# Turning the token rows on VectorE, in blocks of quarter rows, in a gated attention and mixture-of-experts layer on one core

## What is computed

```python
router_logits = flat @ router_w.T
probs = jax.nn.softmax(router_logits, axis=-1)
topk_w, topk_idx = jax.lax.top_k(probs, TOP_K)          # TOP_K = 2 of E = 16 experts
topk_w = topk_w / jnp.sum(topk_w, axis=-1, keepdims=True)
shared = silu(flat @ shared_gate_w) * (flat @ shared_up_w) @ shared_down_w      # F_SH = 1024
...
g = jax.lax.ragged_dot(xs, gate_w, group_sizes)         # D = 1024 -> F_EXP = 512
u = jax.lax.ragged_dot(xs, up_w, group_sizes)
h = silu(g) * u
dn = jax.lax.ragged_dot(h, down_w, group_sizes)         # 512 -> 1024
routed = zeros_like(flat).at[sorted_tok].add(sorted_w[:, None] * dn)
output = shared + routed
```

## Time and profile before

| | |
|---|---|
| median of 3 executions | 3086.06 us |
| the profiled execution, on the device | 3110.33 us |
| its span, from the first to the last instruction | 3108.8 us |
| PE busy | 2960.7 us (95%) |
| DVE busy | 1638.6 us (53%) |
| ACT busy | 1013.8 us (33%) |
| POOL busy | 595.8 us (19%) |
| mean granted TensorE clock | 0.979 of full speed |

### The profile page before, as it was taken

How to read it: one execution, slowest core, us unless ns; L and a number is a source line. 1 busy time by engine, 2 the same in 40 slices (tenths; PEclk the granted TensorE clock), 3 DMA queues, 4 the chain that set the end, 5 groups by cost and what they waited for, 6 DMA issues and landing times.

```text
span 3108.8 us, 48018 instructions
## 1 busy us (share of the span) xinstructions
PE 2960.7 (95%) x17262; PEld 2443.7 (79%) x17263; DVE 1638.6 (53%) x3104; ACT 1013.8 (33%) x1916; POOL 595.8 (19%) x572
## 2 busy tenths in 40 slices
PE   4799999999999988999999999999999999999999
PEld 3687777777878766888888888888888888888887
DVE  3778788887888764333243333332333344444444
ACT  4444444444444412332233333332333331111111
POOL 1333333333343331000000000000000001111111
PEclk6799999999999998999999999999999999999999
DMA  6454445445444534143433333433333324444444
GB/s 192 137 170 137 150 137 176 151 140 158 152 150 142 153 128 152 59 149 128 142 141 136 142 135 142 142 135 142 140 143 135 135 81 158 145 138 159 142 145 145
DMA packets 205721, 441.74 MB, mean 142 GB/s; under 512 B 86784, under 2 KB 87680, under 8 KB 205056
## 3 DMA queue, kind: packets, MB, share of 16 engines
q1 hardware_dynamic: 110544, 333.62, 31.7%
q0 software_dynamic: 24400, 72.96, 7.2%
q10 hardware_dynamic: 70656, 33.56, 4.2%
HBM read 350.72 MB, written 107.18 MB: 147 GB/s over the span
## 4 chain that ended last, share of the span: by engine, by line
PE 59%; DVE 1%; ACT 1%; ACTq 0%; issue 0%; DVEq 0%
PE p_g_b L1532 19%; PE p_up_b L1532 19%; PE p_y_b L1520 17%; PE p_x_b L1500 3%; PE p_h_b L1507 1%; DVE w_lo L1384 1%; ACT w_hi L1327 1%; ACTq L1181 0%; ACTq L1166 0%; DVE x L1440 0%; DVE sg_b L1412 0%; DVE x L1431 0%; ACT th_b L1369 0%; DVE y_b L1442 0%; ACTq L1323 0%
## 5 line engine op out<-in xcount | busy, mean ns | idle before, releaser
L1400 DVE TENSOR_TENSOR ht_lo_b<-p_h_b,ht_hi_b 128x512 fp32r<-128x512 f32 x105 | 72.4, 689 | 544.5 <-ACT ht_hi_b L1339 544.5
L1532 PE MATMUL p_g_b<-w_hi,xt_hi_b 128*128 128x512 f32 x840 | 342.0, 407 | 16.2 <-DVE w_lo L1384 12.9
L1520 PE MATMUL p_y_b<-w_hi,ht_hi_b 128*128 128x512 f32 x840 | 340.1, 405 | 1.9 <-DVE ht_lo_b L1400 1.9
L1412 DVE SCALAR_TENSOR_TENSOR sg_b<-th_b,p_g_b 128x512 f32<-128x512 f32 x105 | 72.1, 687 | 493.5 <-ACT th_b L1369 493.5
L1532 PE MATMUL p_up_b<-w_hi,xt_lo_b 128*128 128x512 f32 x840 | 331.0, 394 | 0.0
L1532 PE MATMUL p_up_b<-w_lo,xt_hi_b 128*128 128x512 f32 x840 | 330.1, 393 | 0.0
L1520 PE MATMUL p_y_b<-w_lo,ht_hi_b 128*128 128x512 f32 x840 | 330.0, 393 | 0.0
L1532 PE MATMUL p_g_b<-w_hi,xt_lo_b 128*128 128x512 f32 x840 | 329.8, 393 | 0.0
L1532 PE MATMUL p_up_b<-w_hi,xt_hi_b 128*128 128x512 f32 x840 | 327.4, 390 | 0.0
L1532 PE MATMUL p_g_b<-w_lo,xt_hi_b 128*128 128x512 f32 x840 | 327.0, 389 | 0.0
L1520 PE MATMUL p_y_b<-w_hi,ht_lo_b 128*128 128x512 f32 x840 | 326.8, 389 | 0.0
(11 more groups left out here) (221 smaller groups left out, 5694.1 us busy)
## 6 DMA issues: line engine op xcount, KB each, us to landing
mid_y<-y_b SPq DMA_DIRECT2D x73, 512.0 KB, 3.2
stage<-mid_g_row SPq DMA_DIRECT2D x64, 512.0 KB, 5.4
stage<-in_eg SPq DMA_DIRECT2D x16, 2048.0 KB
stage<-in_eu SPq DMA_DIRECT2D x16, 2048.0 KB, 15.2
stage<-in_ed SPq DMA_DIRECT2D x16, 2048.0 KB, 19.4
mid_y<-in_x SPq DMA_DIRECT2D x34, 512.0 KB
stage<-in_x SPq DMA_DIRECT2D x32, 512.0 KB
stage<-in_ctx_t ACTq DMA_DIRECT2D x32, 512.0 KB, 8.3
```

Of the source, the lines that this page charges most:

```text
L1400: nc.vector.tensor_tensor(ht_lo[:, :, :], p_h[:, :, :], ht_hi[:, :, :].bitcast(f32), ALU.subtract).then_inc(ht_rdy, 1)
L1412: nc.vector.scalar_tensor_tensor(out=sg[:, :], in0=th[:, :], scalar=1.0, in1=p_g[:, :], op0=ALU.add, op1=ALU.mult).then_inc(silu_step, 1)
L1520: last = nc.tensor.matmul(p_y[n][:, :], a[:, k, :], b[:, GUP + k, w], start=(k == 0 and m == 0), stop=(k == FE // P - 1 and m == 2))
L1532: mm = nc.tensor.matmul(out[:, :], a[:, k, :], w[:, k, o:o + FE], start=(k == 0 and m == 0), stop=(k == KD - 1 and m == 2))
```

## The change

**x.** The eight transposes of PE per tile are gone. A tile's rows are laid in `xg` as quarter rows: the 32 partitions of group a hold quarter a (256 floats) of all 128 tokens, four tokens to a partition. One instruction of DVE (`turn_x`) then turns 32 x 32 blocks inside each group of partitions into a new SBUF tile `x_t`, which is whole. Its row p of block k is column 8p + k of x, so the weights are loaded in the same order ("(p k)" in place of "(k p)"). `x_high` and `x_low` read `x_t` in place of PSUM.

**Gathering x.** POOL loads the numbers of the tokens four times (once for each group of partitions, 32 x 4 numbers), adds 0 to 3 to four times the token's number (`idx_q`; the lists now hold four times the number), and issues four indirect DMAs of 128 quarter rows of 1 KB. The plain loads of x are four DMAs of 32 partitions each (`quarters_in`).

**h.** The gated rows go to memory and back: ACT stores `h` to a DRAM buffer `mid_h` (`h_store`), waits for the store, loads it in the layout of quarters (`h_quarters`), DVE turns it (`turn_h`, in place of PE's), and ACT and DVE split it. Only the very last tile's h is still turned by PE.

**y.** Both halves of y are copied at the start of the next `body` (`y_of`), behind `split_gu` where a tile is an expert's first.

```diff
-        eng.dma_start(place, matrix.rearrange("(k p) f -> p k f", p=P)).then_inc(sem, 16)
+        eng.dma_start(place, matrix.rearrange("(p k) f -> p k f", p=P)).then_inc(sem, 16)
...
+        xn_quarters = t["xn"].rearrange("(c j t) (a d) -> c a j t d", t=4, j=32, a=4)
+        xn_flat = t["xn"].rearrange("c (a d) -> (c a) d", a=4)
+        xg_parts = xg[:, :].rearrange("p (t d) -> p t d", t=4)
+
+        def quarters_in(eng, c, done):
+
+            for a in range(4):
+                eng.dma_start(xg_parts[32 * a:32 * a + 32, :, :], xn_quarters[c, a]).then_inc(done, 16)
...
             def load_x(c):
-                sp.wait_ge(xt_ps, before + c)
-                sp.dma_start(xg[:, :], xn_rows[c]).then_inc(xs_in, 16)
+                sp.wait_ge(x_turned, before + c)
+                quarters_in(sp, c, xs_in)
...
-                    ge_apart(pool, past, (x_in, 16 * i))
-                    pool.dma_start(idx[:, :], list_parts[bass.ds(part, 1)].rearrange("o p w -> (o p) w")
-                                   ).then_inc(idx_in, 16)
-
-                ge_apart(pool, past, (idx_in, 16 * i + 16 if c is None else 0), (xt_ps, i))
+                    for a in range(4):
+                        pool.dma_start(idx[32 * a:32 * a + 32, :],
+                                       list_parts[bass.ds(part, 1)].rearrange("o (j t) w -> (o j) (t w)", t=4)
+                                       ).then_inc(idx_in, 16)
+                    ge_apart(pool, past, (idx_in, 64 * i + 64))
+                    ge_apart(pool, past, (x_in, 64 * i))
+                    nc.gpsimd.tensor_tensor(idx_q[:, :], idx[:, :], quarter[:, :], ALU.add).then_inc(idx_rdy, 1)
+                    ge_apart(pool, past, (idx_rdy, i + 1))
+                ge_apart(pool, past, (x_turned, i))
...
+                    for n in range(4):
+                        nc.gpsimd.indirect_dma_start(
+                            out=xg_parts[:, n, :], out_offset=None, in_=xn_flat,
+                            in_offset=bass.IndirectOffsetOnAxis(ap=idx_q[:, n:n + 1], axis=0)).then_inc(x_in, 16)
...
                 for p in range(GUP):
+                    if p == 3:
+                        h_quarters(i)
                     nc.scalar.activation(w_hi[:, p, :], stage[:, p, :], ACT.Copy).then_inc(gu_hi, 1)
...
+            def h_store(i):
+
+                act.wait_ge(h_rdy, i)
+                act.dma_start(t["h"].rearrange("a s f -> s a f"), h[:, :].rearrange("p (a f) -> p a f", a=4)
+                              ).then_inc(hs_out, 16)
+
+            def h_quarters(i):
+
+                act.wait_ge(hs_out, 16 * i)
+                act.dma_start(h[:, :], t["h"].rearrange("a (j t) f -> (a j) (t f)", t=4)).then_inc(hq_in, 16)
...
+            def y_of(q):
+
+                act.wait_ge(y_out, 16 * q)
                 act.wait_ge(y_ps, 2 * q)
-                nc.scalar.activation(y[:, 512:D], p_y[1][:, :], ACT.Copy).then_inc(y_rdy, 1)
+                for n in range(2):
+                    nc.scalar.activation(y[:, 512 * n:512 * n + 512], p_y[n][:, :], ACT.Copy).then_inc(y_rdy, 1)
...
                 if not (isinstance(i, int) and i < 2) and (c is None or isinstance(c, int) and c < 2):
-                    y_right(q)
+                    y_of(q)
                 if prev:
-                    h_high(i)
+                    if not first:
+                        h_quarters(i)
+                    h_high(i, q)
                 act.wait_ge(gu_ps, i + 1)
                 nc.scalar.activation(th[:, :], p_g[:, :], ACT.Tanh, scale=0.5).then_inc(tanh_rdy, 1)
                 if not last:
                     x_high(i + 1)
-                if prev == "routed":
-                    y_left(q)
+                    h_store(i + 1)
                 if first:
                     split_d(i, e, prev)
...
+            def turn_h(i):
+
+                dve.wait_ge(xt_rdy, 2 * i)
+                dve.wait_ge(hq_in, 16 * i)
+                nc.vector.transpose(h_t[:, :, :].rearrange("p k (j t) -> p t k j", t=4),
+                                    h[:, :].rearrange("p (t i k) -> p t k i", t=4, k=FE // P)).then_inc(h_turned, 1)
...
+            def turn_x(i, c):
+
+                ge(dve, xt_rdy, 2 * i)
+                if c is None or isinstance(c, int) and c == 0:
+                    dve.wait_ge(x_in, 64 * i + 64)
+                else:
+                    dve.wait_ge(xs_in, 64 * c)
+                nc.vector.transpose(x_t[:, :, :].rearrange("p k (j t) -> p t k j", t=4),
+                                    xg_parts[:, :, :].rearrange("p t (i k) -> p t k i", k=KD)).then_inc(x_turned, 1)
...
                 if prev:
-                    h_low(i)
+                    turn_h(i)
+                    h_low(i, h_t)
+                if not last:
+                    turn_x(i + 1, c)
                 silu_up(i)
...
-                    if k == 3 and prev:
-                        turn_h(i)
                 mm.then_inc(gu_ps, 1)
-                if not last:
-                    turn_x(i + 1, c)
                 if prev:
                     down(i, e - 1 if first else e)
```

More of the change, by code:

```diff
@@ L166, in mix_block @@
         cnt_ps, cnt_step = sem("cnt_ps"), sem("cnt_step")
-        idx, idx_in, row0_in = keep["idx"], keep["idx0_in"], keep["row0_in"]
+        idx, idx_q, quarter = keep["idx"], keep["idx_q"], keep["quarter"]
+        idx_in, idx_rdy, row0_in = keep["idx0_in"], keep["idx0_rdy"], keep["row0_in"]
         gu0_hi, gu0_split = keep["gu0_hi"], keep["gu0_split"]
         xn_out = sem("xn_out")
-        fill_in = sem("fill_in")
+        fill_in, quarter_set = sem("fill_in"), sem("quarter_set")
         wp_in = [sem(f"wp_in{n}") for n in range(SLOTS)]
@@ L1131, in ffn_block @@
         base_row = sb("base_row", [P, D])
-        p_x = [ctx.enter_context(nc.psum_tensor(f"p_x{n}_{tag}", [P, 4, P], f32)) for n in range(2)]
         p_g = ctx.enter_context(nc.psum_tensor(f"p_g_{tag}", [P, FE], f32))
@@ L1137, in ffn_block @@
         r0, r1 = keep["x1"][:, 0, :], keep["x1"][:, 1, :]
-        idx, starts_i = keep["idx"], keep["starts_i"]
+        idx, idx_q, quarter, starts_i = keep["idx"], keep["idx_q"], keep["quarter"], keep["starts_i"]
         first_row = sb("first_row", [P, NE])
@@ L1295, in gather @@
                     own = start(pool, NE)
-                    pool.wait_ge(y_out, 16 * own)
+                    pool.wait_ge(y_out, 16 * own + 16)
                     for n in range(2):
@@ L1377, in _ @@
             x_high(0)
-            tiles(act, body, lambda i, q, e, c: h_high(i))
+            tiles(act, body, lambda i, q, e, c: last_high(i))
         @block.vector
@@ L1490, in _ @@
             trio = ((xt_hi, w_hi), (xt_lo, w_hi), (xt_hi, w_lo))
-            def turn_x(i, c):
-                if c is None or isinstance(c, int) and c == 0:
-                    pe.wait_ge(x_in, 16 * i + 16)
-                else:
-                    pe.wait_ge(xs_in, 16 * c)
-                for k in range(KD):
-                    last = nc.tensor.transpose(p_x[k // 4][:, k % 4, :], xg[:, k * P:(k + 1) * P], ident[:, :])
-                last.then_inc(xt_ps, 1)
             def turn_h(i):
@@ L1506, in turn_h @@
                 for k in range(FE // P):
-                    last = nc.tensor.transpose(p_h[:, k, :], h[:, k * P:(k + 1) * P], ident[:, :])
+                    last = nc.tensor.transpose(p_h[:, k, :], h[:, k:FE:FE // P], ident[:, :])
                 last.then_inc(ht_ps, 1)
```

78 lines of the change are left out of this document (45 added, 33 removed).

## The result

The changed kernel takes **3050.6 us** (median of 4 runs, 3043.6 to 3054.7) against 3085.0 us for the kernel before beside it (3082.6 to 3086.2): ratio 0.989, 95% interval 0.9878 to 0.9902. It is faster by 34 us (30 to 38), where 146 were forecast and 2940 us, and the range (2930 to 2990) does not hold it.

A forecast was written before the change was run, and what follows sets the result against it. PE, busy 95% of the span, was taken as the bound. Savings of 89.6 us (x), 45.8 (h) and 12.9 (changes of expert), less 2 (start), made 146 us off the 3086.1 median: 2940 us, range 2930 to 2990.

The forecast's parts named there:

- The PE work that goes: PE's transposes removed per tile: x 0.87 us in 103 tiles, h 0.44 in 104; 89.6 and 45.8 us saved.
- DVE's turn: Turning x and h on DVE in each tile: 1.22 and 0.69 us, at most 2.9 and 1.4, hidden.
- h by way of memory, plain tiles: Store and load of h in routed tiles without a change of expert: 3.2 us each way, hidden.
- the place named the tightest: Tile behind a change of expert: load of h issued late on ACT, may take 3.4 us against 3.2 assumed.
- The first rival: Trip of h late behind a change: 5 us each way, 27 us lost, giving 2967 us; chance 0.12.
- The first of the prediction's signs of being wrong: In plain tiles, PE waiting for DVE's `ht_lo` or `xt_lo` would show the prediction wrong.
- h has ACT's queue to itself: Argument against h's trip being late behind a change while the next expert's 6 MB start.
- The weights' order in memory changes no byte count: nothing: Loads of the expert weights in the new order: claimed to cost nothing.
- The changes keep their 0.8 us: Rival at changes of expert: DVE's first piece a little late, 13 us of gain lost, giving 2953 us.
- The gather: Gather of x by four DMAs in place of one: 9.6 to 12.1 us within a 16.5 us period, hidden.
- The start: POOL's longer chain to tile 0 and DVE's turn there: 2 us lost, at most 5 to 8.
- The rival on the other side, the trip that binds everywhere: Memory trip of h late in all kinds of tiles: at 8.3 us each way 334 us, giving 3274; chance 0.05.

The follow-up runs named there:

- weights apart: Changed kernel, but the next expert's gate matrix is issued once one tile's h has landed, up and down after the next tile's: 2948.1 us, again 2941.2.
- the kernel with both edits: Changed kernel with weights apart, plus ACT's first piece of new weights ahead of the store of h: 2936.1 us, again 2923.4 (ratios 0.9474, 0.9479).
- half of the change alone: Kernel before with the change's handling of h and y and its weight order; x still gathered and turned as before: 3114.3 us, ratio 1.006.
- the runs with mean waits of 3.5 and 2.6 us: 3.5: changed kernel, next expert's weights all issued one tile later, 3021.6 us. 2.6: kernel before with only h and y handling and weight order changed, 3114.3 us.

## Why the prediction was wrong

- **The PE work that goes** was right and somewhat under-sized. A tile takes 16.32 us, not 16.49. What the chain shows of a group of transposes, 0.87 and 0.44 us, leaves out some 0.08 us at its edges: removing them gave 0.95 and 0.53. That is 103 x 0.95 + 104 x 0.53 = 153 us, not 135. The duration of 273 ns for one and the 340 us that would go by it did not come.
- **DVE's turn** was mis-sized by the factor 1.8 and 1.6: 2.22 and 1.11 us for 1.22 and 0.69. It fell inside the bound of 4.3 us a tile, and cost nothing.
- **h by way of memory, plain tiles**: 2.6 us out and 2.7 back where I had 3.2 each; hidden, in the shared tiles too. The load in the tile behind a change was taken to stand behind ACT's split and copies, at T + 10.9. It was issued at T + 6.5 (T = 1540.82), while ACT was at the second of four pieces:

```profile
1546.30 2.01 ACT L1362 ACTIVATE w_hi<-stage 128x1024 fp32r<-128x1024 f32 x2 [2.91 <-PE p_y_b L1576]
1547.28 0.33 ACTq L1373 DMA_DIRECT2D h_b<-mid_h  x1
```

  So the place named the tightest had some 4 us more than was counted.
- **The failed step is the price of the trip under the weights.** "This is the tightest place" named the tile behind a change, and looked at the load of h that ends as the 6 MB begin. They take 20 us from there and so lie over the next tile's store, a place I had counted among the plain ones, with 3.2 us. There the trip took 16.1 us where 16.3 - 2.1 (the store's issue) - 2.7 (turn and splits) = 11.5 were allowed, so PE was 4.6 us late, and its clock fell on top: 108 us over 15 experts in place of nothing. The first rival had the cause right (0.12) but put it in the tile behind the change, took 5 us a way and priced it at 27 us. The first of the prediction's signs of being wrong, PE waiting for `ht_lo` in tiles that it counted as plain, is what came. The trace of before held the warning, under its own weights:

```profile
mid_y<-y_b SPq DMA_DIRECT2D x1, 512.0 KB, 8.6
xn<-mid_xn,idx POOLq DMA_INDIRECT x1, 7.3
```

  These are the landings in 1575 to 1600 us. I took the medians of the earlier trace rows, 3.2 and 4.4, in which one tile in four does not show. Against it I had put "h has ACT's queue to itself": the runs show that a queue of one's own does not protect: 12.8 us under a load from SP's queue, 2.6 without it. The Trainium skill, DMA: Bandwidth & Descriptors (Queues, rings and completion order), has each DMA engine take turns between queues by the packet, where a packet is a group of descriptors and not one piece of the kind counted here. The trace shows no turns; it agrees in that fewer pieces of h (6.4 for 12.8 us) and smaller ones of the weights (9.1) both let the store land sooner.
- **"The weights' order in memory changes no byte count: nothing"** is wrong by some 16 to 22 us, by the packets and not the bytes.
- **The changes keep their 0.8 us** (15.6 us against 12.9), a rival of its own. I gave ACT 0.56 us to get going; behind the store's issue it needs 1.6 (1525.66 to 1527.25), with the register loads in between, so its first piece starts at T + 4.1 (1527.25), where I had it end. Taking it ahead of the store gained 18 to 22 us: the idle time and the slow first product behind it (0.50 us for 0.23).
- **The gather** is hidden, as said: with h on TensorE, PE waits for nothing in the routed stage.
- **The start** costs some 6 us and not 2: from the last up product of the attention stage to the first gate product it is 11.0 us (1178.7 to 1189.7) for 7.0 (1203.0 to 1210.0), and tile 1 follows 17.9 us behind tile 0 (1207.58 - 1189.71) for 15.7 (1225.65 - 1209.99).

Together: 153 - 6 - 108 - 3 = 36 us, where the runs show 34 (30 to 38). For weights apart they are 153 - 6 - 3 = 144, measured 143 and 136. For the kernel with both edits the same terms, 153 - 6 + 13 + 4 (the slow first product at 16 changes), make 164, measured 160. The rival on the other side, the trip that binds everywhere, did not come about; half of the change alone is slower than before too, but by the stalls behind the weights.

## What to carry to other kernels

Price a new trip through memory in the tile in which the largest other transfer is under way, all through that transfer and not only at its start: take the worst landing in such a window of the trace, not the median. When a large prefetch has slack, cut it into pieces and start each behind the small latency-bound transfer of its tile: here two waits on SP's queue turned 34 us of gain into some 140. And ahead of an engine's first piece of urgent work nothing should stand that waits, not even the issue of a DMA.

## What the runs showed of the hardware

- A store of 256 KB in 512 pieces of 512 bytes landed in 2.6 us alone and in 12.8 to 14.4 under a load of 6 MB from another queue; in 128 pieces of 2 KB it landed in 6.4 under the same load, and its load in 512 pieces took 7.9.
- A turn of 128 x 1024 fp32 on DVE took 2224 ns with strides of 8 elements between neighbours in and 4 out, and 1237 in plain order; 128 x 512 took 1109 with strides of 4 and 707 without. The Trainium skill, Vector Engine (DVE) Microarchitecture Reference (The reshape front-end and per-opcode configuration), has a transpose sustain one element per cycle per lane. In plain order the second 512 elements cost 530 ns (1237 - 707), 1.04 ns each, as in DVE's plain passes over the same shapes (1218 and some 690 ns), which fits that; the strided order does not.
- Behind PE's wait of 4.6 us the granted clock was 0.57 for 4 us, and 24 products took 7.35 us in place of 5.44; behind all 15 waits of the changed kernel they took 7.05 to 8.59. In the runs with mean waits of 3.5 and 2.6 us they were slow in 12 of 15 places each. I had not priced this.
- A DMA issue on ACT's queue went out at 1547.28 us, while four activations that stand ahead of it in program order, two of them copies of y at 1550.11, were still to start.
- The attention stage, the same code, ended between 1177 and 1203 us in fourteen profiled executions. Where a change lies in another stage, the stage's own time is the finer measure.
